# Block transposes on VectorE around the attention division, and four buffers of normalized queries filled up to three slots ahead

## The reference

```python
q = layernorm(x)                                     # 256 queries, 16 heads of 16
u = einsum('hbqd,hbkd->hbqk', heads(q), heads(ctx)) * scale / sqrt(16)
attn = softmax(where(mask, -inf, tanh(u) * exp(log_C)))
x = x + merge(attn @ heads(ctx)) @ W_out.T
f = layernorm(x)
gf = global_net(mean(f))                             # 3 small layers per batch
out = f
for _ in range(3):
    tf = coupling_net(out)                           # 256 -> 256 -> 128 -> 64 -> 1, gelu, sigmoid
    out = out + coupling(gf, tf) * twist(out)        # twist permutes and negates quarters
x = x + out
```

## Time and profile before

| | us |
|---|---|
| median of three runs (lowest, highest) | 1159.69 (1159.38, 1160.45) |
| time of the profiled execution | 1161.73 |
| its span, first to last instruction | 1159.9 |
| PE busy | 1060.9 (91%) |
| ACT busy | 932.9 (80%) |
| DVE busy | 793.8 (68%) |
| POOL busy | 579.1 (50%) |

### The profile page before, as it was taken

How to read it: one execution, slowest core, us unless ns; L and a number is a source line. 1 busy time by engine, 2 the same in 40 slices (tenths; PEclk the granted TensorE clock), 3 DMA queues, 4 the chain that set the end, 5 groups by cost and what they waited for, 6 DMA issues and landing times.

```text
span 1159.9 us, 23508 instructions
## 1 busy us (share of the span) xinstructions
PE 1060.9 (91%) x8028; PEld 604.0 (52%) x8028; DVE 793.8 (68%) x1738; ACT 932.9 (80%) x1153; POOL 579.1 (50%) x1117
## 2 busy tenths in 40 slices
PE   6899989999899998999999998999989999898894
PEld 4566436654466544665356643665436654465331
DVE  4777486866778576874868749587486866675285
ACT  5899778996799877988779877799778987695576
POOL 4466206881078711796037940489206881175303
PEclk8999999999999999999999999999999999998897
DMA  4110001220022100221012200022001220010002
GB/s 128 46 42 19 1 2 46 69 68 1 2 69 69 47 1 1 69 68 46 1 24 69 69 23 2 25 86 65 8 1 47 68 68 1 2 42 29 18 1 74
DMA packets 67286, 43.95 MB, mean 38 GB/s; under 512 B 42080, under 2 KB 50784, under 8 KB 67168
## 3 DMA queue, kind: packets, MB, share of 16 engines
q1 hardware_dynamic: 67168, 42.45, 12.7%
HBM read 25.51 MB, written 16.78 MB: 36 GB/s over the span
## 4 chain that ended last, share of the span: by engine, by line
PE 49%; DVE 15%; POOL 14%; ACT 11%; issue 9%; SPq 1%; DMA 1%; DVEq 0%; POOLq 0%; ACTq 0%
PE ps L1143 7%; PE ps L1065 7%; PE ps L1156 7%; PE ps L1111 6%; ACT probs L833 6%; PE ps L1169 5%; PE ps L1081 4%; DVE move_u L725 3%; PE ps L1090 3%; POOL q_hat L403 2%; DVE coup L691 2%; PE ps L1199 2%; POOL f_hl L498 2%; DVE f_t L729 2%; DVE move_u L704 2%
## 5 line engine op out<-in xcount | busy, mean ns | idle before, releaser
L833 ACT ACTIVATE probs<-ps,u_scale 120x2048 f32<-120x2048 f32 x128 | 251.3, 1963 | 37.1 <-PE ps L1065 37.0
L839 ACT ACTIVATE probs<-probs,exp_bias,clip 120x2048 f32<-120x2048 f32 x128 | 267.1, 2087 | 0.1
L1169 PE MATMUL ps<-h,w 128*128 128x512 f32 x384 | 184.2, 605 | 13.9 <-ACT h L865 13.1
L447 POOL TENSOR_TENSOR c<-tok_c 128x16 f32<-128x16 f32 x8 | 1.8, 221 | 328.8 <-issue 328.8
L1065 PE MATMUL ps<-q_t,k_t 32*120 32x256 f32 x2048 | 146.9, 400 | 12.7 <-ACT probs L833 11.9
L636 DVE COPY o_t<-ps 128x512 f32<-128x512 f32 x128 | 88.4, 690 | 94.8 <-PE ps L1081 94.8
L1111 PE MATMUL ps<-wo_t,of_t 128*128 128x256 f32 x512 | 140.8, 398 | 3.1 <-DVE of_t L656 3.1
L1081 PE MATMUL ps<-probs,va 120*32 120x256 f32 x2048 | 138.6, 389 | 1.0 <-DVE o_tok L649 1.0
L498 POOL TENSOR_TENSOR f_hl<-f_t,f_hl 128x512 f16<-128x512 f32 x64 | 73.4, 1156 | 82.3 <-DVE f_hl L682 82.3
L1065 PEld LDWEIGHTS ps<-q_t,k_t 32*120 32x120 f32 x2048 | 92.6, 178 | 40.7 <-issue 35.8
L1169 PEld LDWEIGHTS ps<-h,w 128*128 128x128 f32 x384 | 66.8, 188 | 89.4 <-issue 64.3
(11 more groups left out here) (133 smaller groups left out, 2024.1 us busy)
## 6 DMA issues: line engine op xcount, KB each, us to landing
xy<-in_x_dram SPq DMA_DIRECT2D x64, 256.0 KB, 2.8
out_dram<-xy SPq DMA_DIRECT2D x64, 256.0 KB, 2.0
cbuf<-in_ctx_dram SPq DMA_DIRECT2D x64, 120.0 KB, 2.6
tok_c<-coup SPq DMA_DIRECT2D x256, 0.5 KB, 2.0
move_v<-in_L_xattn_W_out_dram SPq DMA_DIRECT2D x1, 256.0 KB, 5.5
move_u<-in_L_ffn_cn_w_dram SPq DMA_DIRECT2D x1, 256.0 KB, 5.9
w<-in_L_ffn_cn_w_dram SPq DMA_DIRECT2D x1, 128.0 KB, 5.8
g<-in_L_ffn_gc_w_dram SPq DMA_DIRECT2D x1, 128.0 KB, 4.2
```

What stands on the lines that cost most here:

```text
L833: eng.activation(probs[:, b % 2, n * HALF:(n + 1) * HALF, :].rearrange("k h q -> k (h q)"), banks(SCORE_BANK, 4)[0:KEYS, :], ACT.Tanh, sca ...
L839: eng.activation(p, p, ACT.Exp, scale=clip[0:KEYS, 0:1], bias=exp_bias[:, b:b + 1]).then_inc(s_exp, 1)
L1169: last = eng.matmul(banks(bank), w2[:, k, :], h1[:, p % 2, k, :], start=(k == 0), stop=(k == EK - 1))
```

## The change

Around the division: `attn_out` becomes a DVE transpose of 32 x 32 blocks from PSUM to `o_t`; a head's 16 values and its sum fill one block, so `divide` can work on `o_t` in SBUF at once; `attn_features` becomes a second block transpose from the quotient `o_n` to `of_t`. `attn_to_tokens` and `attn_to_features` of PE are gone, and heads are dealt to the value banks in another order. Waits on the removed steps move to `s_ot`, `s_on` and `project`.

Around the queries: four buffers of `q_hat` and its statistics (`QR`). In the ffn three batches are normalized instead of one, in slots 0, 1 and 4 none, in slots 2 and 3 batch i+3, in 5 to 7 batch i+2 as before. The load of the third of those batches moves from slot 0 into the ffn. `query_hat`, `norm_2` and `factors` are cut in two each (`query_scale`, `norm_2_scale`, `twisted_part` and `x_part`) and interleaved.

```diff
+        def ahead_in_slot(i):
+            if i < GROUP + LAG:
+                return i + 2 if i >= 0 else None
+            at = (i - LAG) % GROUP
+            return None if at in (0, 1, 4) else i + 3 if at < 4 else i + 2
+        def ahead_in_ffn(g):
+            early = g * GROUP + GROUP + LAG
+            return [b for b in range(early + 2, early + 5) if b < NB]
...
                 if kind != "attention":
+                    for b in ahead_in_ffn(i)[2:]:
+                        load(b)
                     coupling_rows(i)
...
-                elif 0 <= i + 4 < NB and i >= -1:
+                elif 0 <= i + 4 < NB and i >= -1 and not after_ffn(i):
                     load(i + 4)
...
+                new = ahead_in_slot(i)
                 if 0 <= i - LAG < NB:
+                    norm_2_scale(i - LAG)
+                    if after_ffn(i):
+                        norm_2(i - LAG)
+                        coefficients(groups_before(i) - 1)
+                for b in late[:1]:
+                    twisted_part(b)
+                if 0 <= i - LAG < NB and not after_ffn(i):
                     norm_2(i - LAG)
-                if i == early:
-                    coefficients((i - LAG) // GROUP - 1)
+                if new is not None and 2 <= new < NB:
+                    query_scale(new)
                 for b in late[:1]:
-                    factors(b)
+                    x_part(b)
...
             def attn_out(b, n):
                 eng.wait_ge(s_pv, 2 * b + n + 1)
                 if b >= 2:
-                    eng.wait_ge(s_otr, b - 1)
-                eng.tensor_copy(o_t[:, b % 2, 2 * n:2 * n + 2, :].rearrange("p c q -> p (c q)"),
-                                banks(PV_BANKS[n])).then_inc(s_ot, 1)
+                    eng.wait_ge(s_on, b - 1)
+                eng.transpose(o_t[:, b % 2, 2 * n:2 * n + 2].rearrange("p c q r -> p (c q r)"),
+                              banks(PV_BANKS[n])).then_inc(s_ot, 1)
...
-                eng.wait_ge(s_otr, b + 1)
-                eng.reciprocal(inv_sum[:], heads[:, :, :, DH]).then_inc(s_inv, 1)
+                eng.wait_ge(s_ot, 2 * (b + 1))
+                eng.reciprocal(inv_sum[:], o_t[:, b % 2, :, :, DH]).then_inc(s_inv, 1)
...
-                eng.tensor_tensor(o_tok[:].rearrange("p t (h d) -> p t h d", d=DH), heads[:, :, :, 0:DH],
-                                  inv_sum[:].unsqueeze(3).to_broadcast([P, TT, H, DH]), ALU.mult).then_inc(s_otok, 1)
+                eng.tensor_tensor(o_n[:].rearrange("p q k a d -> p (k a) q d"), o_t[:, b % 2, :, :, 0:DH],
+                                  inv_sum[:].unsqueeze(3).to_broadcast([P, NG, QB, DH]), ALU.mult).then_inc(s_on, 1)
...
             def attn_features(b):
-                eng.wait_ge(s_oftr, b + 1)
+                eng.wait_ge(s_on, b + 1)
                 if b:
                     eng.wait_ge(s_proj, TT * b)
-                eng.tensor_copy(of_t[:].rearrange("p k q -> p (k q)"), banks(X_BANK)).then_inc(s_oft, 1)
+                eng.transpose(of_t[:].rearrange("p k (q i) -> p q k i", i=SQ),
+                              o_n[:].rearrange("p q k a d -> p q k (a d)")).then_inc(s_oft, 1)
```

More of the change, by code:

```diff
@@ L413, in values, with norm_2_scale @@
                                   1.0, None, ALU.mult).then_inc(s_va, 1)
-            def norm_2(b):
+            def norm_2_scale(b):
                 at = b % XR
@@ L422, in norm_2 @@
                 eng.tensor_tensor(rstd2[:, at, :], var2[:, b % 2, :], minus_half[:], ALU.pow).then_inc(s_rstd2, 1)
+            def norm_2(b):
+                at = b % XR
                 eng.wait_ge(s_neg2, b + 1)
@@ L499, in low_half @@
                    .then_inc(s_flo, 1)
-            early, late = None, []
+            late = []
             for kind, i in slots():
                 if kind == "ffn":
-                    early = i * GROUP + GROUP + LAG
-                    if early + 2 < NB:
-                        query_hat(early + 2)
+                    for b in ahead_in_ffn(i):
+                        query_scale(b)
+                        query_hat(b)
                     for chunk in (2, 3):
@@ L520, in _ @@
                     values(i + 1)
-                if i == -2:
-                    query_hat(0)
-                    query_hat(1)
-                elif 2 <= i + 2 < NB and i != early:
-                    query_hat(i + 2)
+                if new is not None and 2 <= new < NB:
+                    query_hat(new)
                 if i >= LAG and (i - LAG) % GROUP in LOW_AT:
@@ L755, in end_combine @@
                    .then_inc(s_res, 1)
-            late, early = [], None
+            late = []
             for kind, i in slots():
@@ L761, in _ @@
                 if kind == "attention":
-                    new, nxt, here, old = i + 2, i + 1, i - 1, i - 2
+                    new, nxt, here, old = ahead_in_slot(i), i + 1, i - 1, i - 2
                     if i == -2:
@@ L773, in _ @@
                         keys_out(nxt)
-                    if 2 <= new < NB and i != early:
+                    if new is not None and 2 <= new < NB:
                         stats(new)
@@ L793, in _ @@
                 else:
-                    early = i * GROUP + GROUP + LAG
-                    if early + 2 < NB:
-                        stats(early + 2)
+                    for b in ahead_in_ffn(i):
+                        stats(b)
                     high_half(i, 2)
@@ L1237, in _ @@
                         weighted_values(here, 0)
-                    if 0 <= old < NB:
-                        attn_to_features(old)
                     if 0 <= nxt < NB:
@@ L1251, in _ @@
                         project(old, 1)
-                    if 0 <= here < NB:
-                        attn_to_tokens(here)
                     if 0 <= i - LAG < NB:
```

101 lines of the change are left out of this document (48 added, 53 removed).

## The result

The changed kernel takes 1163.59 us (median of 17 runs, 1161.49 to 1167.48), the kernel before in the same comparison 1161.1 (17 runs, 1159.03 to 1162.6): ratio 1.003, 95% interval 1.0022 to 1.0038. It is slower by 0.3% where I forecast 1135.5.

A forecast was written before the change was run, and what follows sets the result against it. Attention slots were taken as bound by PE and ACT chasing each other, then by POOL from slot 3's high half; gains of 2.8, 19.8 and 1.6 sum to 24.2 us, giving 1135.5 us, range 1119 to 1158.

The forecast's parts named there:

- The prices: DVE's block transposes were priced near a copy of the same 512 elements (0.68 us), at 0.05 us more.
- Rival 1: Block transposes on DVE are slow, 0.6 us over a copy, in every slot: 1204 us, chance 0.12.
- The loop of DVE and PE: In free attention slots, DVE with one PE step was to bound the slot at 8.6 us, gaining 0.4.
- ACT's floor: In attention slots, ACT alone could run a slot in 8.41 us.
- The seven slots ahead of the first ffn: Attention slots before the first ffn were to gain 0.4 us each, 2.8 in all.
- the margin of 0.9 us at the ffn's entry: Second low halves ready at 403.4, PE needing them at 404.30; thin cover, counted at nothing.
- rival 2: POOL and the ffn's entry eat the gain: third load and low halves late, contention at its most; 1150 us, chance 0.11.
- Rival 3: PE's clock falls in attention slots, six us more a slot; one in eight falling gives 1180 us, chance 0.05.
- the split of `norm_2`: In POOL's slot, `f_hat` comes two large instructions (1.1 us) later, before PE asks for it; counted at nothing.
- the waits saved: In POOL's stretch, the 0.17 us wait between `rstd` and its user goes five times, 0.9 us.
- The end of slot 7: After its queries, slot 7 was to run to its end without PE's detours, gaining 0.6 us a round.
- Contention: DVE's multiply with both inputs in SBUF, and shifted collisions, were to lengthen POOL's stretch by 1.8 us.

The follow-up runs named there:

- e3: Changed kernel with chunk 2's high half (DVE) and low halves (POOL) behind the first of three query batches in the ffn: 1147.28 us, ratio 0.988.
- e11: Changed kernel with SP's load ahead of the store in each attention slot, nothing else: 1142.44 us, ratio 0.9855.
- e13: Kernel before the change with SP's load ahead of the store in each attention slot, nothing else: 1160.25 us, ratio 1.0001.
- e15: Changed kernel with load ahead of store, chunk 2's halves after the ffn's first query, POOL's old order, and four idle-time matmuls in slot 7 alone: 1138.79 us, ratio 0.9805.
- e4: Changed kernel with four extra identity matmuls on PE in each attention slot, ahead of the queries: 1153.67 us, ratio 0.9943.
- e1: Kernel before the change with the new division alone (block transposes, no PE transposes), queries as before: 1152.5 us, ratio 0.9929.
- e9: Changed kernel with chunk 2's halves after the ffn's first query and POOL's old order, no added matmuls: 1141.42 us, ratio 0.9833.
- e12: Changed kernel with POOL's slot in its old order (second normalization, factors, values, whole query), nothing else: 1153.08 us, ratio 0.9943.
- e8: e5 with the four low halves in slots 4 to 7 instead of 3 to 6: 1154.06 us, ratio 0.9949.
- e14: e11 with four idle-time identity matmuls of PE in slot 7 alone: 1143.85 us, ratio 0.9847.
- e6: e5 with the reciprocals written to PSUM from batch 4 on, so the multiply reads one SBUF operand: 1148.91 us, ratio 0.9905.
- e7: e5 with POOL's slot in its old order, nothing interleaved: 1141.61 us, ratio 0.9838.
- e5: Changed kernel with chunk 2's halves after the ffn's first query and four idle-time matmuls in each attention slot: 1148.11 us, ratio 0.9889.

## Why the prediction was wrong

**The prices were right.** Block transposes take 0.71 and 0.67 us beside a copy's 0.65 to 0.69. The Trainium skill, page "Vector Engine (DVE) Microarchitecture Reference", section 3.8, has the transposing array sustain one element per cycle per lane; the rows agree so far as a transpose costs no more than a copy of as many elements. Rival 1 fell.

**The loop of DVE and PE was sized too long.** I put a free slot at 8.6; it is 8.38, ACT's floor (forecast 8.41). The seven slots ahead of the first ffn gave 4.2 instead of 2.8. The other 1.8 of the start lie in its slots 1 and 2 (18.6 us instead of 20.4), and are not settled: the kernel before with the moved load began its first round at 179.9, not 177.9.

**The step that failed first: the margin of 0.9 us at the ffn's entry, which I counted at nothing.** The sum for it kept the store at its old place and looked only at the third load. That load landed 5.5 us after the store was issued, where I had 5.0 (by its own terms, 2.0 and 2.8, 4.8). But the second load stands behind the same store, so POOL's second query ended 7.5 us after the store and the third could not start when its statistics were there, 6.5 after it. The first two low halves took 2.7 instead of 2.3 and were ready 12.6 to 12.7 after the store, where I had 10.7. And the store itself came 0.7 us later in the round, 1.1 instead of 1.8 ahead of the ffn's start, so PE asked 11.0 after it, where I had 11.6. From 0.9 to spare it went to 1.6 to 1.8 short, which is PE's wait of 1.66 to 1.85. Six ffns lost 10.7 us. The sentence in rival 2 that PE reaches this point no earlier was right (9.8 and 9.9 us after the ffn's start); it did not save the margin, since the other side moved. e3 shows this place: with the low halves ahead of the second query PE doesn't wait. e11 shows that the store ahead of the second load makes most of it, and e13 that this order costs nothing before the change. What makes the store later was not tested; it is 1.1 to 1.3 ahead with the division alone and 1.5 with the queries alone.

**The second: PE's idle time was counted as free.** Rival 3 had the clock fall for a whole slot at 6 us. What fell was 2 to 4 us at a time, at 0.9 to 1.7 us a time, some 8.6 us in six rounds: slot 7 three times 1.45, slot 0 0.93, slots 1 and 2 together twice 1.7. In the tail a stretch of 8 us was granted 0.50, where the lowest of before was 0.70; what this cost is not shown, as e15 has such a stretch too and a tail 4.4 us shorter. That the clock is what cost it in the slots is shown by e4: more PE work, no fall, 10 us less, of it 6.0 in the slots. The gap of slot 7 is the clearest case. Seven versions have the gap unfilled (the changed kernel, e1, e3, e9 to e12), and 22 of their 42 slots 7 have a fall; in the seven with the matmuls in it (e4 to e8, e14, e15) none of 42 has. Before the change the transposes stood in that gap.

**The third: the interleaving on POOL, of which I counted the split of `norm_2` at nothing and the waits saved as 0.9 us of gain.** Slots 3 to 6 took 36.7 us instead of the forecast 36.05 (before 37.96); with the old order alone (e12) they take 35.9, though the waits of 0.17 are back. That is 0.8 a round, 4.7 in all. In the round of the rows above, `f_hat` of slot 4 was ready 7.8 us after T, past the 6.4 at which I had PE ask for it, and PE waited 0.25 for it (e12: ready at 6.3). In slot 6 `f_hat` was ready 0.4 us before PE came to it; there the query came 0.2 later, 1.4 instead of 1.2 after T. ACT's waits of 0.81 and 0.53 in these slots are only in part new: the kernel before has 0.51 and 0.62.

**The end of slot 7 gave nothing instead of 0.6 a round.** Its queries come 39.4 us after slot 3's T, not 38.2, and 2.8 after its own T where it was 2.1. What PE saved there it waited.

**Contention was real and cost little or nothing.** I took 1.8 us a round, 10.8 in all. e6 takes 18.7 us of busy time from DVE and POOL (the multiply 51.2 to 44.3, combine 48.8 to 53.3, POOL's three large groups 235.6 to 219.3) and the time does not move; up to some 4 us may be hidden there, as said.

The miss of 24.4 us in the profile, worked out: ffns 10.7; slots 13.1, of it the clock 8.6; tail 3.8; start -3.3. With these repaired (e15) the gain is 21 us, near the sum of 24.2. That it comes so near is in part luck: the start gave 6.2 instead of 2.8 and slots 1 and 2 gave 7.2 instead of 4.8. The loss was in three places that I had put at nothing.

**What stays open.** Which slot the clock falls in. Filling slot 7 moved the falls to slots 0 and 1 in e14, and not in e15; e9 has seven, five of them in slot 7, and is no slower than e7 with none. Falls in slots 3 to 6 come in e1, e3, e8, e9 and e15, so filling slot 7 is no full cure, and e5 and e8 show the same of matmuls in every slot. The same wait of 1.9 us is followed by a fall in one round and not in the next. What makes slots 0 and 1 fall is not shown either: PE's wait of 0.73 us ahead of the fall in slot 0 stands in all six slots 0 of the changed kernel, of which one falls, and in e11's, of which none does. So that e11 lost no time in slots 0 and 1 is its result, but that the load's place caused it is only inferred: 8.0 of its 19.1 us, the ffns', is what the trace ties to the load.

## What to carry to other kernels

Where a change takes work from an engine, look at what that engine waits for just after, and give each margin under 2 us a price. Check both of its ends: here PE asked at the same point of the ffn as before, and the margin went because the store, and all that stood behind it, came 0.7 us later and in a longer row. Read the order in a DMA queue as a chain: a store that waits for a computation delays each load behind it, which costs nothing until someone asks for that load one slot sooner. Two rivals can come true together, as the entry and the clock did here, so sum their losses and don't only rank them.

## What the chip showed that I had not expected

With PE idle for some 1.9 us in the midst of dense work, the granted clock fell in three of six slots 7: some 4 us at 0.56 to 0.59, and sixteen matmuls took 2.08 us instead of 1.14. Four otherwise useless matmuls of 1.16 us together in the gap kept it at 1.00 in all 42 slots 7 of seven versions. A VectorE multiply of 128 x 512 elements took 0.80 us in the mean with both operands in SBUF beside a busy GpSimd and 0.69 with the small operand in PSUM, and GpSimd's last factor step went from 0.64 to 0.55.
